# A second copy of the attention values, context turns spread over three groups, weight units sent through DRAM, and four idle products per attention group

## What is computed

```python
q, k, v = x @ wq.T + bq, x @ wk.T + bk, x @ wv.T + bv     # 32 heads of 16
scores  = einsum('bshd,bstd->bsht', q, k) / 4             # per token: head against head, 32 x 32
context = einsum('bsht,bstd->bshd', softmax(scores), v)
x1      = layernorm(x + context)
dq1, dq2, dq3 = nf4(w1), nf4(w2), nf4(w3)                 # quantised and dequantised, blocks of 64
out     = layernorm(x1 + (silu(x1 @ dq1.T) * (x1 @ dq2.T)) @ dq3.T)   # hidden size 1376
```

## Time and profile before

| | before |
|---|---|
| median of 3 runs | 901.09 us (899.78 to 904.98) |
| profiled execution, its time | 904.12 us |
| profiled execution, span of the core | 902.0 us |
| PE / DVE / ACT busy | 736.6 / 642.2 / 469.5 us |
| mean granted TensorE clock | 0.81 |
| moved by DMA | 103.15 MB |

### The profile page before, as it was taken

One profiled execution on the slowest core, in us unless ns is written; L12 is line 12 of the kernel. 1 busy time (PEld: TensorE's weight loads), 2 busy tenths in 40 slices (PEclk: granted clock), 3 DMA queues, 4 the chain that ended last, 5 costly groups with the idle time before them and its releaser, 6 DMA issues.

```text
span 902.0 us, 13969 instructions
## 1 busy us (share of the span) xinstructions
PE 736.6 (82%) x5668; PEld 627.5 (70%) x5668; DVE 642.2 (71%) x878; ACT 469.5 (52%) x599; POOL 20.8 (2%) x48
## 2 busy tenths in 40 slices
PE   2989999704676765966996998897989999999994
PEld 2767787603676764956885887786868888877883
DVE  1479898616748647758776689999999988634443
ACT  2287887523532533544552686677767655512212
POOL 0010000000000000000000000000000000000000
PEclk9999999955555555555555999999989999999997
DMA  9943453898866989779062230311303112113314
GB/s 188 222 136 100 144 154 117 189 164 138 172 108 92 159 167 159 121 173 150 24 211 93 89 122 26 118 45 72 118 17 111 44 68 94 60 49 111 122 33 93
DMA packets 68319, 103.15 MB, mean 114 GB/s; under 512 B 22496, under 2 KB 51680, under 8 KB 65184
## 3 DMA queue, kind: packets, MB, share of 16 engines
q1 hardware_dynamic: 68256, 102.26, 48.4%
HBM read 72.10 MB, written 30.15 MB: 113 GB/s over the span
## 4 chain that ended last, share of the span: by engine, by line
PE 53%; DVE 19%; DMA 12%; issue 9%; ACT 4%; SPq 2%; ACTq 0%; DVEq 0%
PE ps_p L791 12%; DVE nf_acc L929 9%; DMA v_bd<-v_blocks 7%; PE ps_p L707 6%; PE ps_s L707 6%; PE ps_s L708 6%; PE ps_s L709 6%; PE ps_p L709 6%; PE ps_p L708 6%; PE ps_s L778 3%; DMA qk_parts<-qk_p 2%; ACT nf_y L561 1%; DMA v_blocks<-v_t 1%; SPq L422 1%; DMA k_st<-qk_parts 1%
## 5 line engine op out<-in xcount | busy, mean ns | idle before, releaser
L929 DVE SCALAR_TENSOR_TENSOR nf_acc<-nf_y,nf_acc 128x1024 f32<-128x1024 f32 (+3 forms) x238 | 286.8, 1205 | 50.2 <-ACT nf_y L561 42.8
L561 ACT ACTIVATE nf_y<-nf_w,bound_b 128x1024 f32<-128x1024 f32 (+3 forms) x255 | 281.0, 1131 | 10.0 <-DVE nf_acc L929 6.6
L791 PE MATMUL ps_p<-probT,v_bd 128*68 128x32 f32 x1024 | 126.4, 304 | 43.8 <-DMA v_bd<-v_blocks 32.0
L791 PEld LDWEIGHTS ps_p<-probT,v_bd 128*68 128x68 f32 x1024 | 122.4, 210 | 46.3 <-DMA v_bd<-v_blocks 33.1
L707 PE MATMUL ps_s<-x_hl,f_ha 128*128 128x512 f32 (+1 forms) x224 | 88.1, 393 | 0.0
L708 PE MATMUL ps_s<-x_hl,f_ha 128*128 128x512 f32 (+1 forms) x224 | 87.8, 392 | 0.0
L709 PE MATMUL ps_s<-x_hl,f_la 128*128 128x512 f32 (+1 forms) x224 | 87.7, 391 | 0.0
L778 PE MATMUL ps_s<-k_st,q_st 96*32 96x32 bf16 x2048 | 44.3, 249 | 51.1 <-DMA k_st<-qk_parts 26.5
L707 PE MATMUL ps_p<-x_hl,w_hl 128*128 128x512 f32 x192 | 77.6, 404 | 3.0 <-DVE x_hl L949 1.3
L1095 DVE TENSOR_TENSOR silu<-silu,ps_s 128x512 f32<-128x512 f32 (+1 forms) x44 | 30.1, 684 | 69.4 <-PE ps_s L709 69.4
L778 PEld LDWEIGHTS ps_s<-k_st,q_st 96*32 96x32 bf16 x2048 | 39.9, 171 | 55.7 <-issue 53.3
(11 more groups left out here) (90 smaller groups left out, 1176.3 us busy)
## 6 DMA issues: line engine op xcount, KB each, us to landing
x_hl<-x_parts SPq DMA_DIRECT2D x12, 2048.0 KB, 8.1
qk_parts<-qk_p SPq DMA_DIRECT2D x64, 204.0 KB, 2.5
x_parts<-x_st SPq DMA_DIRECT2D x16, 512.0 KB, 4.4
q_st<-qk_parts SPq DMA_DIRECT2D x8, 816.0 KB, 9.7
k_st<-qk_parts SPq DMA_DIRECT2D x8, 816.0 KB, 18.4
nf_w<-in_L_ffn_w SPq DMA_DIRECT2D x24, 256.0 KB, 3.2
q_st<-qk_parts SPq DMA_DIRECT2D x8, 544.0 KB, 11.8
k_st<-qk_parts SPq DMA_DIRECT2D x8, 544.0 KB, 20.7
```

The costliest lines, as they stand in the source:

```text
L561: act.activation(nf_y[0:p, at % NY, 0:w], nf_w[0:p, u % 2, 0:w], ACT.Identity, bias=bound_b[0:p, i:i + 1], scale=STEEP).then_inc(s_ny, 1)
L791: t = pe.matmul(ps_p[0:MV, (3, 0)[G % 2], i * H:(i + 1) * H], v_bd[:, :, g * GI + i], probT[:, G % 2, i], start=True, stop=True)
L929: dve.scalar_tensor_tensor(out=acc, in0=y, scalar=float(NF4[i + 1]), in1=acc, op0=ALU.min, op1=ALU.max).then_inc(s_nacc, 1)
```

## The change

- `v_bd` gets two buffers with rows of 72 instead of 64 elements. The values of half h+1 are loaded at the second group of half h, once those of half h-1 are used up.
- `qk_p` has 6 slots instead of 3, `v_t` 4 instead of 2. `ps_p` gives the products of the values four banks instead of two.
- The five context turns stand in three groups (10, 11, 12; likewise 18.. and 26..), the moments in the third, the normalisation in the next and the `xt` turns in the two after.
- A unit is scaled into `nf_st`, stored to DRAM (`dequantised`), and loaded again into the place of its low half, from which PE turns it. Six units are reloaded near the end of the attention, the others one step behind the step they are finished in, and turned another step later.
- Levels: 59, 55 and then 141, with five in every step.
- The weights of the projections are issued on ACT's queue instead of SP's.
- In each group from the third on, `fill` issues four bf16 products of 512 columns and 32 rows of output, into rows of `ps_p` that nobody reads.

```diff
-    LV_P = [1, 1, 1, 1, 1, 1, 1, 1, 1, 2, 1, 2] * NBK
-    LV_P[:4] = [0] * 4
+    LV_P = [1, 1, 1, 1, 1, 1, 1, 1, 1, 2, 2, 2] * NBK
+    LV_P[:4] = [0, 1, 1, 1]
     LV_A = [2] * GG
-    LV_F = [(2, 2)] * (8 * NJG) + [(0, 0)] * (NS - 8 * NJG)
-    LV_F[:2] = [(0, 2)] * 2
-    LV_F[2] = (0, 4)
-    LV_F[4:20] = [(2, 3)] * 16
+    for b in range(NBK - 1):
+        LV_A[8 * b + 10:8 * b + 13] = [1, 1, 1]
+    LV_F = [(2, 3)] * (8 * NJG) + [(0, 0)] * (NS - 8 * NJG)
...
+            def store_unit(u):
+                sp.wait_ge(s_dq, u + 1)
+                sp.dma_start(dq_d[u, 0:parts_of(u), 0:width(u)], nf_st[0:parts_of(u), 0:width(u)]).then_inc(s_dst, 16)
...
+            def reload(u):
+
+                kind, g, k = UNITS[u]
+                sp.wait_ge(s_dst, 16 * (u + 1))
...
             for G in range(GG):
                 hb, g = divmod(G, NG)
+                store_units(G - len(LV_A))
                 levels(LV_A[G])
-                if g == 1 and hb:
-                    sp.wait_ge(s_pv, NG * hb)
-                    values_stored(sp, KC * (hb // 2 + 1))
-                    load_v(hb)
+                if g == 1 and hb + 1 < NHB:
+                    if hb:
+                        sp.wait_ge(s_pv, NG * hb)
+                    else:
+                        sp.wait_ge(s_vzero, 2 + 2 * Q4)
+                    values_stored(sp, KC * ((hb + 1) // 2 + 1))
+                    load_v(hb + 1)
...
+            def fill(G):
+
+                hb = G // NG
+                if G % NG == 0:
+                    pe.wait_ge(s_ldv[hb % 2], 16 * Q4 * (hb // 2 + 1))
+                wait(pe, s_ctx, G - NPV + 1)
+                some = v_bd[hb % 2][:].bitcast(BF16)
+                for _ in range(FILL):
+                    pe.matmul(ps_p[96:128, (G + 3) % NPV].rearrange("p (a t) -> p a t", t=TI), some[:, 0, 1:TI:2],
+                              some[:, 0:8, 1:2 * TI:2], start=True, stop=True)
...
             for G in range(GG):
                 scores(G)
-                if G in CT_AT:
-                    for k in range(len(HEADS)):
-                        turn(("ct", CT_AT[G], k))
+                for key in CT_AT.get(G, []):
+                    turn(key)
                 if G >= 2:
+                    fill(G - 2)
                     values(G - 2)
```

More of the change, by code:

```diff
@@ L146, in layer_kernel @@
         while len(finished) < NU and done >= LEVELS * (len(finished) + 1):
-            finished[len(finished)] = at - len(LV_P) - len(LV_A)
-    for u in range(len(finished), NU):
-        finished[u] = 8 * NJG
+            finished.append(at - len(LV_P) - len(LV_A))
+    assert len(finished) == NU and finished[NU0 - 1] < -4
+    RELOAD_AT = {}
     at = 2
@@ L152, in layer_kernel @@
         g = UNITS[u][1]
[L153 to L158, removed]
+        at = max(at, finished[u] + 2, NBK * NJG + 2 if g == 2 else 0)
+        if len(F_TURNS.get(at, [])) >= 2:
+            at += 1
+        F_TURNS[at] = [("f", u, s) for s in range(2)]
+        RELOAD_AT.setdefault(max(finished[u] + 1, 0 if g == 1 else NBK * NJG + 1), []).append(u)
     for s in range(NS):
@@ L276, in layer_kernel @@
         s_dq = sem("s_dq")
+        s_dst = sem("s_dst")
+        s_rld = [sem(f"s_rld{u}") for u in range(NU)]
         s_ldx = [sem(f"s_ldx{i}") for i in range(2)]
@@ L480, in _ @@
                     load_stack(1, hb + 2)
+                if G == GG - NG:
+                    sp.wait_ge(s_score, GG - NG)
+                    for u in T_UNITS + W_UNITS:
+                        reload(u)
                 for key in XT_AT.get(G, []):
@@ L505, in _ @@
                 g, b, j = STEPS[s]
+                store_units(s)
                 levels(sum(LV_F[s]))
+                if s == 0:
+                    sp.wait_ge(s_pv, GG)
+                if s == NBK * NJG + 1:
+                    sp.wait_ge(s_sum, Q4 * NBK)
+                for u in RELOAD_AT.get(s, []):
+                    reload(u)
                 for key in F_TURNS.get(s, []):
@@ L534, in _ @@
             pool.wait_ge(s_tr, TURN[("w", 2, KC - 1)] + 1)
-            pool.memset(v_bd[:], 0.0).then_inc(s_vzero, 1)
-            pool.wait_ge(s_vzero, 1)
-            for q in range(Q4):
-                pool.memset(v_bd[32 * q:32 * q + 32, DV * q + D], 1.0).then_inc(s_vzero, 1)
+            for slot in range(2):
+                if slot:
+                    pool.wait_ge(s_vzero, 1 + Q4)
+                    pool.wait_ge(s_ql, 2 * KC * NBK)
+                    parts_stored(pool, 2 * KC * NBK)
+                    values_stored(pool, KC * NBK)
+                pool.memset(v_bd[slot][:], 0.0).then_inc(s_vzero, 1)
+                pool.wait_ge(s_vzero, (1 + Q4) * slot + 1)
+                for q in range(Q4):
+                    pool.memset(v_bd[slot][32 * q:32 * q + 32, DV * q + D], 1.0).then_inc(s_vzero, 1)
             for b in range(NBK):
@@ L663, in _ @@
             for G in range(GG):
-                if G >= 3:
-                    context(G - 3)
+                for at in CONTEXT_AT.get(G, []):
+                    context(at)
                 steep(LV_A[G] // 2)
@@ L1056, in _ @@
                 low(key)
-            add_context(NBK - 1)
+            for k in range(len(HEADS)):
+                add_context(("ct", NBK - 1, k))
             moments(NBK - 1)
```

234 lines of the change are left out of this document (134 added, 100 removed).

## The result

| | before | after |
|---|---|---|
| median | 900.77 us (899.78 to 904.98, 4 runs) | 916.19 us (914.07 to 917.72, 4 runs) |
| profiled execution, its time / span | 904.12 / 902.0 us | 915.51 / 913.7 us |
| PE / DVE / ACT busy | 736.6 / 642.2 / 469.5 us | 799.8 / 643.2 / 471.9 us |
| mean granted TensorE clock | 0.81 | 0.83 |
| moved by DMA | 103.15 MB | 120.29 MB |

What follows compares the result with a forecast made beforehand. No engine is full, so the stage decides: PE in the projection, PE and DVE nearly level in the attention, DVE then PE in the feed-forward. Terms -5 - 2 - 6 - 1 + 9 + 1 = -4 gave 897 us, range 874 to 916.

Steps and rivals of the forecast that it cites:

- The whole term: Start and projection: slots, clock and weights' queue gain, seven added levels cost; sum -5 us, bounds -8 and +3.
- if that cover were gone: Projection: if DVE's free time didn't hide the seven added levels, they would cost the whole +8.4 us instead of +1.5.
- The gains of the six slots: Projection: six `qk_p` slots remove a PE idle, -3.1 us, and about -2 for the clock and waits behind it.
- The prediction's own sign for hidden levels that aren't hidden: Projection: over 150 us from its first product would mean that the 7 levels were not hidden.
- The attention's total: Attention: half of the groups at either clock, between 272 and 238 us, so 255 us, -6.
- the low clock's 272 us: Attention, all at low clock: 234.4 us PE busy with `fill`, 35.1 of issue, plus 2; 272 us, +11.
- 238 is the floor for any speed of the engines: Attention: 201 us of DMA, 8 of added stores and some 27 for the last half, rounded up to 238 us.
- what is late next is the stack: Attention: with the values' wait gone, PE's first waits for `k_st` would come at the start of halves 2 to 7.
- Feed-forward: Feed-forward: five levels in all steps until the 141 are done, +9 us, and late reloads through DRAM, +1.
- that rival: Feed-forward: the path through DRAM is late, 11 later units each hold PE some 2 us; 917 us, chance 0.08.
- the clock stays down: Attention: `fill` costs 1.7 us in each group at low clock, +11; whole kernel +14, 915 us, chance 0.20.
- the opposite rival: The clock stays up from the first groups: attention at its floor, -23, tail -3; 878 us, chance 0.34.

Runs made afterwards that it cites:

- the best kernel: The changed kernel without idle products, doubled projection levels in places 8, 10 and 12, and `v_bd` rows of 64: 874.38 us, ratio 0.9692; run again, 873.24 us.

## Why the prediction was wrong

It was wrong by 19 us and in sign, and 916.2 us lies just outside the stated range, which ended at 916. The forecast had the projection 5 us shorter, and it became 10.5 us longer: these 15.5 us are the largest miss of all terms. Point by point:

- **The step that failed: "At 1.2 us each they are 8.4 us of DVE work, and DVE has 14.9 us free here. I charge +1.5."** The whole term was -5, with +3 as the bound, and it came out at +10.5. The free time was a mean over the stage, but the doubled levels stood where DVE had none: ahead of the last low half of the next block. Three waits of 3.0 us and some 6 us of clock behind them come to 15 us, from which what was gained elsewhere in the stage goes off. The same 59 levels in other places take 9.3 us less, with waits that are shorter and a clock that stays up. Even "if that cover were gone", with the whole +8.4, the term would have been +2; the clock's part was left out. The gains of the six slots were charged too high as well: with the levels in a good place the projection still ended 1.2 us later than before, though the waits for `qk_p` were gone. Nor did the weights' own queue give 1.5 us: the first product started at 26.75 us, against 25.93 before. The prediction's own sign for hidden levels that aren't hidden came up: the projection took 158 us from its first product, over the 150 named.
- **The attention's total was right (-7.2 against -6), by two errors that cancel.** The clock was to be high for half of the groups; it was 0.58 on the mean, just under the 0.6 named, which between 0.50 and 1.00 means about a sixth of the time. And the high clock was to shorten values and scores "by something between nothing and half". It is next to nothing: 4.29 and 4.32 us for the values. So a high-clock group isn't 4 us, but 6.7. On the other side the low clock's 272 us kept all 35.1 us of issue waits beside the added work; 15.4 of them vanished under it. The work itself was right: 234.4 us forecast for the low clock, 233.4 measured. That the sum came out was luck. The `fill` itself was sized right, 1.7 us low and 0.9 high against 1.88 and 1.07.
- **"238 is the floor for any speed of the engines" was wrong.** The attention took 226.3 us without the idle products, at a DMA share of 0.91. That is 206 us of DMA work, near the 201 + 8 of the working. What failed is the 27 us at the end in which DMA was to have little to do: there its share was 0.71, with the reloads among it, where it was 0.22 before. With that floor in mind the products looked nearly free, since DMA would have held the stage anyway; they cost 28.7 us. The alternative "the same kernel without them" was never worked out, and it is what the change should have been measured against.
- **The wait for the values** went, as forecast, and the run with late values shows that the early load did it. Between those two kernels it is worth 42.9 us, against the kernel before rather the 32.0 us. The context turns' wait went too, but it was worth little. The term "what is late next is the stack" was wrong: no wait for a stack came.
- **Tail: +5.1 against -1.** PE's timeline shows four pieces, all ahead of the last context turns; from these on the tail takes 16.3 us in both kernels. One set of four idle products stands behind the last scores (1.8 us). Three groups of values are slower (1.2 us together). The last pair of x1 turns moved one group back and so behind the last scores (1.8 us). The rest is some 0.4 us of waiting: 1.26 us for the copy of `ctx` are new, and others are gone. The change had named the first and the third, and the working charged neither. Without the idle products the tail took 37.6 us, and in the best kernel 36.3 us.
- **The rows of 72** were named in the change and charged nothing. They cost 4 to 5 us in the changed kernel; without the idle products the attention gained nothing from taking them back, and no run there separates them from the levels (the two together gave 13.1 us).
- **Feed-forward: +4.5 against +10.** Steps 0 to 31, from the silu of step 0 to that of step 32, took 293.5 us against 288.3, where the working had 297 and 288. The mechanism was right, the size too large, 5.2 us for these steps instead of 9: steps 0 to 22 took 9.54 us each (219.4/23), and the next nine 8.23. The reloads through DRAM were hidden in this kernel. Three other tables of levels show that rival at work, mostly with the trigger that the prediction named, a load of x1 ahead on the queue. It costs at one to three units, though, not at eleven.
- **Which rival came true?** By the number "the clock stays down" (915 us, 0.20), but not by its terms: it had +11 for the attention, which gave -7.2, and -5 for the projection, which took +10.5. Its clock was the nearest to what came, but 915 us was hit by luck. The reason given for the opposite rival, "steps of 9.69 us with 15% idle keep 0.97", rests on a misreading: PE is busy 140.84 of 155.00 us there, so 9% is idle. The Trainium skill ("TensorE: Matmul & The Clock Gate", Part 1, the HAM clock gate) has sustained activity release the clock. The rows agree in direction only: 0.51 before, 0.58 with four products a group, 0.70 with eight. With PE busy 92% of the stage it was mostly 1.2 GHz.

The change holds one large gain, the early load of the values, and three losses that can be taken out one by one. Without them it is 873 to 874 us, 3.1% faster than the kernel before. Of the 29.8 us between the two profiled executions (902.0 and 872.2 us) the attention gives 34.9 and the wait for the first stack 1.0; the tail takes 2.1 back and the feed-forward 4.1.

What is left in that attention are 50.1 us of issue waits at a DMA share of 0.94. Their places show a pattern. PE in the best kernel, and over the same stage the larger of the two queues that the profile calls instruction queues (packets, MB, share):

```profile
212.81 0.83 PE L844 MATMUL ps_s<-k_st,q_st 96*32 96x32 bf16 x34 [8.89 <-issue]
213.57 3.96 PE L868 MATMUL ps_p<-probT,v_bd 128*68 128x32 f32 x32
217.46 1.30 PE L844 MATMUL ps_s<-k_st,q_st 96*32 96x32 bf16 x61
225.41 0.26 PE L844 MATMUL ps_s<-k_st,q_st 96*32 96x32 bf16 x3 [6.64 <-issue]
...
q8 instruction: 25, 0.41, 0.9%
```

Between the two waits stand 34 + 32 + 61 = 127 products. In the kernel before the counts and the places in the program are the same, with waits of 7.74 and 5.25 us. There are 12 issue waits in this stage, and each but the first stands one, two or three times 126 to 128 products behind the one ahead of it. The stage has 3113 products, each with a weight load, and 25 packets of some 16 KB came on the instruction queue: 125 products a packet. PE has no such wait in the projection or the feed-forward, where the mean DMA share is 0.5 or less and 127 products of 512 columns take some 29 us, against some 7 us here. That fits a PE that runs out of loaded instructions while the DMA engines are full of data. It would also explain why the waits shrink with the idle products, which put more time between two such places. No run has tested it, by fewer PE instructions or by holding data back at those places, so it stays argued.

## What to carry to other kernels

Free time of an engine that is given as a mean over a stage doesn't say that there is room at one place: before work is added, look at what stands behind it on that engine, and who waits. Work that is added only to raise a clock should be priced against the kernel without it, and by rows of the same instructions at both clocks, since instructions that don't shorten gain nothing. On a queue that works in order, a round trip through DRAM is hidden or not by what large load stands ahead of it, and by how soon the reader comes for it, so a table that moves work by a step can cost 5 us. And before two waits are added up as two gains, look whether one stands over the other.

## What the hardware showed that wasn't expected

- The values (float32 products of 32 columns with a weight load of 68 columns each) and the scores (bf16, 32 columns) take the same time at 2.4 and 1.2 GHz: 4.29 and 4.32 us a group, 1.33 and 1.34 us. Four products of 512 columns take 1.07 and 1.88 us.
- A weight load that takes one float32 of each row takes 225 ns with rows of 288 bytes and 210 ns with rows of 256 (means of 1024 loads).
- A wait of PE of 3.0 us in the projection was followed by up to 6 us at the low clock, and a wait of 1.56 us at the same place by none.
- "Issue" waits of up to 8.9 us add up to 50.1 us in the attention of the best kernel, and stand one, two or three times 126 to 128 products apart. With the idle products they are 19.7 us in the changed kernel.
